# The adapter stage written out batch by batch, the initial semaphore values given by four engines, and the first expert's weight split moved to ScalarE and POOL during the selection

## The reference

```python
h = relu(einsum('bsh,bha->bsa', x, W1[lang]) + b1[lang])
x = x + einsum('bsa,bah->bsh', h, W2[lang]) + b2[lang]
n = (x - mean) * rsqrt(var + 1e-5) * gamma[lang] + beta[lang]
S = swapaxes(softmax(einsum('bse,ke->bsk', n, Wg)), 1, 2)
G, I = top_k(S, 128)          # tokens of each expert and batch
```

## Time and profile before

| | |
|---|---|
| Median of 3 runs | 1161.78 us (1161.07 to 1163.18) |
| Profiled execution | 1164.59 us, its span 1162.9 us |
| PE busy | 943.9 us, 81% |
| DVE busy | 746.9 us, 64% |
| POOL busy | 655.6 us, 56% |
| ACT busy | 469.0 us, 40% |

### The profile page before, as it was taken

One profiled execution on the slowest core, in us unless ns is written; L12 is line 12 of the kernel. 1 busy time (PEld: TensorE's weight loads), 2 busy tenths in 40 slices (PEclk: granted clock), 3 DMA queues, 4 the chain that ended last, 5 costly groups with the idle time before them and its releaser, 6 DMA issues. The chain is left out here.

```text
span 1162.9 us, 15224 instructions
## 1 busy us (share of the span) xinstructions
PE 943.9 (81%) x4616; PEld 683.2 (59%) x4616; DVE 746.9 (64%) x1525; ACT 469.0 (40%) x843; POOL 655.6 (56%) x480
## 2 busy tenths in 40 slices
PE   5975049999999999999457999888777888888870
PEld 2764039988998999886123554454454455555550
DVE  2443836666666676652487999999874766667620
ACT  1331126445545644543355657675522222222230
POOL 1010043545545554631899999999930477777771
PEclk9786569999999999998788999999976999999995
DMA  2355732445435433322222332442344599999957
GB/s 70 100 165 179 262 131 55 96 96 104 94 80 117 90 90 78 47 36 103 42 83 109 120 90 91 149 132 82 134 144 141 163 250 246 245 244 257 254 80 153
DMA packets 90450, 151.22 MB, mean 130 GB/s; under 512 B 15816, under 2 KB 72848, under 8 KB 87248
## 3 DMA queue, kind: packets, MB, share of 16 engines
q1 hardware_dynamic: 55184, 95.46, 25.9%
q0 software_dynamic: 25104, 39.86, 18.5%
q10 hardware_dynamic: 10096, 15.10, 3.9%
HBM read 115.37 MB, written 43.42 MB: 137 GB/s over the span
## 5 line engine op out<-in xcount | busy, mean ns | idle before, releaser
L843 ACT ACTIVATE h_raw<-bank,b 128x512 f32<-128x512 f32 x128 | 88.1, 688 | 169.4 <-PE bank L1600 167.1
L1188 DVE TENSOR_TENSOR h_lo<-h_raw,h_hi 128x512 fp32r<-128x512 f32 x128 | 87.2, 692 | 94.9 <-ACT h_hi L847 94.9
L1615 PE MATMUL bank<-w_hi,h_hi 128*128 128x256 f32 x512 | 144.5, 282 | 0.1
L1615 PE MATMUL bank<-w_lo,h_hi 128*128 128x256 f32 x512 | 142.4, 278 | 0.0
L1615 PE MATMUL bank<-w_hi,h_lo 128*128 128x256 f32 x512 | 142.3, 278 | 0.0
L1233 DVE TENSOR_TENSOR_SCAN body<-bank,body 128x512 f32<-128x512 f32 x112 | 130.9, 1211 | 16.7 <-POOL body L610 16.7
L584 POOL DMA_INDIRECT x_rows<-ob,put x64 | 110.6, 1728 | 27.5 <-issue 14.4
L618 POOL TENSOR_TENSOR acc<-acc,body 128x1024 f32<-128x1024 f32 x46 | 108.3, 2354 | 11.7 <-issue 8.2
L1600 PE MATMUL bank<-ex_hi,w_hi 128*128 128x512 f32 x256 | 100.7, 393 | 4.9 <-issue 4.9
L1600 PE MATMUL bank<-ex_hi,w_lo 128*128 128x512 f32 x256 | 101.8, 398 | 0.0
L1600 PE MATMUL bank<-ex_lo,w_hi 128*128 128x512 f32 x256 | 101.5, 396 | 0.0
(11 more groups left out here) (232 smaller groups left out, 2141.5 us busy)
## 6 DMA issues: line engine op xcount, KB each, us to landing
body<-in_mwp SPq DMA_DIRECT2D x46, 512.0 KB, 4.2
head<-in_mwp SPq DMA_DIRECT2D x18, 512.0 KB, 4.1
w1s<-in_fW SPq DMA_DIRECT2D x8, 1024.0 KB, 4.9
w2s<-in_fW SPq DMA_DIRECT2D x8, 1024.0 KB, 5.4
md<-m_rows SPq DMA_DIRECT2D x8, 1024.0 KB, 5.8
body<-m_rows SPq DMA_DIRECT2D x8, 1024.0 KB, 4.8
z_rows<-zrow SPq DMA_DIRECT2D x8, 640.0 KB, 7.1
xt<-in_x SPq DMA_DIRECT2D x8, 512.0 KB
```

The costliest lines, as they stand in the source:

```text
L843: A.activation(h1_raw[f % 4][:, :], bank[:, 2 + f % 4, :], ACT.Gelu_apprx_tanh, bias=b1_0[:, bass.ds(e, 1), f]).then_inc(b_h, 1)
L1188: V.tensor_tensor(h1_lo[:, f, :], h1_raw[f % 4][:, :], h1_hi[:, f, :].bitcast(F32), ALU.subtract).then_inc(b_lo, 1)
L1615: o = T.matmul(rows4(6)[:, j, :], x[:, f, rows], w[q][:, f * H:(f + 1) * H], start=(f == 0 and n == 0), stop=(f == FT0 - 1 and n == 2))
```

## The change

In the adapter stage the loops are gone: every engine has the steps of the 8 batches written out. TensorE's order becomes hidden(b), logits(b-2), adapted(b), input transposes(b+1), back transposes(b-1). VectorE's becomes logits copy(b-2), add and statistics(b), normalise(b), with the row bases of the indices computed in batch 2. ScalarE's becomes ReLU(b), copy of the transposes(b+1), gamma and beta(b-1), store(b-1). The loads of a batch are counted by two semaphores: `a_x` for the tokens, for which the input transposes wait, and `a_in` for the six small tensors, for which hidden waits. The increments of a counter `tally` (`settle`), for which nothing waits, are gone in this stage.

The credits are given by four engines: VectorE the 19 of the a_ semaphores, ahead of everything else it does; ScalarE the 18 of b_, behind its first two DMAs; TensorE the 47 of c_, ahead of its first wait; POOL the 16 of e_, behind its constants.

For the first expert, ScalarE writes the high parts right behind the Exp, ahead of the 22 loads, and POOL subtracts for the low parts, ahead of its wait for the index tables.

```diff
-        a_in = [sem(f"a_in{p}", 16 * 7) for p in range(2)]
+        a_x = [sem(f"a_x{p}", 16) for p in range(2)]
+        a_in = [sem(f"a_in{p}", 16 * 6) for p in range(2)]
...
+        def grant(eng, lo, hi):
+
+            for s, per in credited[lo:hi]:
+                eng.sem_inc(s, CREDIT * per)
...
             G = nc.gpsimd
-            for s, per in credited:
-                pool.sem_inc(s, CREDIT * per)
             G.memset(ident[:, :], 0.0)
...
             pool.drain().then_inc(consts, 1)
+            grant(pool, credits[2], len(credited))
...
-            with pool.Fori(0, B // 2) as i:
-                a_pow(i, 0)
-                a_pow(i, 1)
+            for b in range(B):
+                a_pow(b)
+
+
+            for first in (True, False):
+                src, hi, lo, up, split = ((w1s, w1_hi, w1_lo, b_w1h, b_w1l) if first else
+                                          (w2s, w2_hi, w2_lo, b_w2h, b_w2l))
+                pool.wait_ge(up, level(3))
+                G.tensor_tensor(lo[0][:, :], src[:, :], hi[0][:, :].bitcast(F32), ALU.subtract).then_inc(split, 1)
...
+            grant(act, credits[0], credits[1])
...
+            a_xT_out(0)
+            for b in range(B):
+                a_front(b)
+                if b + 1 < B:
+                    a_xT_out(b + 1)
+                if b:
+                    a_back(b - 1)
+                    a_store(b - 1)
+            a_back(B - 1)
+            a_store(B - 1)
...
             A.activation(lg0[:, :, :, :], lg0[:, :, :, :], ACT.Exp).then_inc(k_exp, 1)
+
+            for first in (True, False):
+                src, dst, came, split = ((w1s, w1_hi, b_w1, b_w1h) if first else (w2s, w2_hi, b_w2, b_w2h))
+                act.wait_ge(came, level(0, 16 if first else 32))
+                for n in range(4):
+                    A.activation(dst[0][:, n * 512:(n + 1) * 512], src[:, n * 512:(n + 1) * 512], ACT.Copy).then_inc(split, 1)
...
+            grant(dve, 0, credits[0])
             V.memset(zeros[:, :], 0.0).then_inc(zeros_set, 1)
...
+            for b in range(B):
+                if b > 1:
+                    a_logits(b - 2)
+                a_front(b)
+                if b == 2:
+                    row_bases()
+                a_norm(b)
+            a_logits(B - 2)
+            a_logits(B - 1)
...
+            grant(pe, credits[1], credits[2])
             pe.wait_ge(ident_set, 1)
...
+            a_xT_in(0)
+            for b in range(B):
+                a_hidden(b)
+                if b > 1:
+                    a_logits(b - 2)
+                a_adapted(b)
+                if b + 1 < B:
+                    a_xT_in(b + 1)
+                if b:
+                    a_backT(b - 1)
+            a_logits(B - 2)
+            a_backT(B - 1)
+            a_logits(B - 1)
```

More of the change, by code:

```diff
@@ L749, in a_store @@
                 act.wait_ge(a_nrm, level(b))
[L750 to L768, removed]
+                act.dma_start(n0_rows[b * S:(b + 1) * S, :].rearrange("(t p) c -> p t c", p=P), nrm[p][:, :, :]).then_inc(a_stored[p], 16)
+            a_xT_out(0)
[6 more added lines that the diff above has]
+                    a_store(b - 1)
@@ L809, in _ @@
             assert n == N_LOADED1
[L812 to L816, removed]
             WC = CT * FF0 // 4
@@ L1063, in a_norm, with a_logits, row_bases @@
                 o.then_inc(a_nrm, 1)
-            def a_logits(h, p):
-                b = 2 * h + p
+            def a_logits(b):
                 dve.wait_ge(a_lgm, level(b))
[L1068 to L1088, removed]
+                V.tensor_copy(lg0[:, b, :, :].rearrange("p t e -> p (t e)"), bank[:, 7, 0:TT * E0]).then_inc(a_lg, 1)
+            def row_bases():
+                dve.wait_ge(consts, 1)
+                V.tensor_scalar(rowbase[:, :], rowbase[:, :], -S, None, ALU.bitwise_and)
+                dve.drain()
+                V.tensor_copy(rowbase_f[:, :], rowbase[:, :])
+                dve.drain()
+                V.tensor_scalar(rowbase_f[B * E0:P, :], rowbase_f[B * E0:P, :], float(S // 2 - B * S), None, ALU.add)
+            for b in range(B):
[7 more added lines that the diff above has]
+            a_logits(B - 1)
             lgf = lg0[:, :, :, :].rearrange("p b t e -> p (b t) e")
@@ L1134, in _ @@
             dve.drain().then_inc(k_tab, 1)
[L1137 to L1140, removed]
-                V.tensor_tensor(lo[0][:, :], src[:, :], hi[0][:, :].bitcast(F32), ALU.subtract).then_inc(split, 1)
             WC = CT * FF0 // 4
@@ L1495, in _, with a_xT_in @@
             T = nc.tensor
+            grant(pe, credits[1], credits[2])
             pe.wait_ge(ident_set, 1)
             pe.wait_ge(loaded0, 16 * N_CONST0)
-            def a_xT_in(h, p):
-                b = 2 * h + p
-                pe.wait_ge(a_in[p], level(h, 16 * 7))
+            def a_xT_in(b):
+                p = b % 2
+                pe.wait_ge(a_x[p], level(b // 2, 16))
                 pe.wait_ge(a_xT, level(b - 1))
@@ L1507, in a_xT_in, with a_hidden @@
                 o.then_inc(a_xTm, 1)
-            def a_hidden(h, p):
-                b = 2 * h + p
+            def a_hidden(b):
+                p = b % 2
+                pe.wait_ge(a_in[p], level(b // 2, 16 * 6))
                 pe.wait_ge(a_xT, level(b))
@@ L1523, in a_adapted, with a_backT @@
                 o.then_inc(a_ad, 1)
-            def a_backT(h, p):
-                b = 2 * h + p
+            def a_backT(b):
+                p = b % 2
                 pe.wait_ge(a_nrm, level(b))
@@ L1542, in a_logits @@
                 o.then_inc(a_lgm, 1)
-            def a_both(h, p, last=False):
-                a_hidden(h, p)
-                a_backT(*prev(h, p))
-                a_adapted(h, p)
-                if not last:
-                    a_xT_in(*nxt(h, p))
-                a_logits(*prev(h, p))
-            def a_first():
-                a_xT_in(0, 0)
-                a_hidden(0, 0)
-                a_adapted(0, 0)
-                a_xT_in(0, 1)
-            def a_last():
-                a_backT(B // 2 - 1, 1)
-                a_logits(B // 2 - 1, 1)
-            adapters(pe, a_first, a_both, a_last)
+            a_xT_in(0)
+            for b in range(B):
+                a_hidden(b)
[9 more added lines that the diff above has]
+            a_logits(B - 1)
             pe.wait_ge(consts, 1)
```

62 lines of the change are left out of this document (28 added, 34 removed).

## The result

The changed kernel took 1132.39 us (4 runs, 1131.0 to 1132.99), the kernel before 1162.48 (4 runs, 1161.07 to 1168.4) beside it: ratio 0.9733, 95% interval 0.9700 to 0.9765. I had forecast 1138.3, a ratio of 0.980 to the 1161.78 of that time, and a range of 1132 to 1150. As a ratio its lower end is 0.9744, and the measured 0.9733 lies just under it. The direction and the three places were right, the gain was called too small. Over all occasions the runs of the kernel before lay between 1154.8 and 1170.7, so the closeness of the four runs on either side says little.

The account below looks back on a forecast made before the run. Everything waits for the expert stage's first product at 162.59 us, so gains before it count in full. 19.2 in the adapters plus 4.3 at the hand-over make 23.5, taking the median 1161.78 to 1138.3; range with rivals 1132 to 1150.

Parts of the forecast that it names:

- y(0) to y(1): Adapter stage, interval between the first two batches' adds: 10.3 us, allowing up to two batches for the clock's first rise.
- The start: Start of the adapters: first transposes wait for the tokens alone, at 7.7 instead of 10.39, 2.7 us gained (0 to 3).
- The cadence: Adapter batches in the new order: 7.7 us on TensorE with the clock up, taken as 8.0 (7.7 to 9.5).
- The third limit: Adapter stage, SP's loads of the tokens: the loop round them takes 15.9 us for two batches, 8.0 each.
- Once up the clock should stay up: Adapter stage: without the wait for a normalisation the clock stays up to the stage's end, five intervals of 8.0 us.
- The tail: From y(7) to the selection: 12.5 us instead of 14.38, by row bases moved (-0.67) and half the clock gain (-1.2).
- The hand-over: Index lists to first product: index copy, first gather, hand-over and last gather shorter, -4.3 us (-2.2 to -4.5).
- The rest: Behind the first product: nothing seen tied to another clock, so no change, 1000.3 us.
- rival 1: Adapter stage: the clock is late or falls again, two more batches at 13.4 instead of 7.7, +11.4 us, 1149.7; chance 0.17.
- POOL did not slow the loop: Selection: a rival had POOL's subtractions block VectorE's loop of max, find and replace, 9.4 us, 1147.7; chance 0.05.
- the clock never stayed down through the stage: Adapter stage: a rival had the clock down throughout, making the kernel slower, +11.1 us, 1172.9; chance 0.03.
- the loads did not set the pace: Adapter stage: a rival had the loads set the pace, 9.5 us a batch, 7.5 us more, 1145.8; chance 0.08.

Follow-up runs that it names:

- e5: The changed kernel measured and profiled again without any edit, against the kernel before: ratio 0.9768, median 1134.81 us.
- e12: The changed kernel a third time without any edit, against the kernel before: ratio 0.9771, median 1136.49 us.
- e3: The changed kernel with POOL giving all initial values again and the first expert's split in its old place (adapter part alone), against the kernel before: ratio 0.9816, 1143.84 us.
- e11: The changed kernel with tokens loaded ahead of the language id and TensorE's 47 initial values given by POOL, against the kernel before: ratio 0.9763, 1137.45 us.
- e4: The changed kernel with the old order of steps on TensorE, ScalarE and VectorE, all else kept, against the kernel before: ratio 0.9874, 1150.25 us.
- e6: The kernel before once more without any edit, for its profile: 1164.03 us (one run).
- e1: The kernel before with only the first expert's split moved (high parts behind the Exp, low parts on POOL), against the kernel before: ratio 0.9950, 1156.76 us.
- e8: The changed kernel with unread products, input transposes(b+1) between hidden and adapted, logits(b-2) last, language id read earlier, against the kernel before: ratio 0.9843, 1142.51 us.
- e10: Like e9, but TensorE's order is hidden(b), input transposes(b+1), adapted(b), back transposes(b-1), logits(b-2); against the kernel before: ratio 0.9743, 1134.62 us.
- e2: The kernel before with only the initial values spread over four engines, against the kernel before: ratio 1.0002, 1163.18 us.
- e9: The changed kernel with tokens loaded ahead of the language id, TensorE's 47 values given by POOL and a few unread products, against the kernel before: ratio 0.9693, 1127.98 us.

## Why the prediction came out too small

By its own steps, before the profile of after:

| step | forecast | first profile | e5 | e12 |
|---|---|---|---|---|
| first transposes | 7.7 | 8.31 | 8.31 | 8.31 |
| y(0) | 19.0 | 17.86 | 19.64 | 17.86 |
| y(0) to y(1) | 10.3 | 6.70 | 9.29 | 6.71 |
| y(1) to y(2) | 9.7 | 9.56 | 7.65 | 8.45 |
| y(2) to y(7) | 40.0 | 40.01 | 41.19 | 41.01 |
| y(7) to the selection | 12.5 | 14.03 | 13.80 | 14.03 |
| selection starts | 91.5 | 88.16 | 91.57 | 88.06 |
| hand-over | 15.7 | 15.23 | 15.1 | 15.2 |
| rest | 1000.3 | 996.0 | 992.4 | 998.0 |

**The step that failed** is "I read its rises as coming out of hidden matmuls and allow up to two batches for the first: that puts y(0) to y(1) at 10.3". In the first profile the clock was up when the adapted matmuls of batch 0 began (1.99 us at 15.83, against 3.62 in the earlier trace rows), so y(0) came 1.1 early and y(1) another 3.6: an interval of 6.70 instead of 10.3. e5 is the case that I had priced, and its stage starts at 91.57, where I had put 91.5; that this is so close is luck, since its intervals miss by up to 2 us either way (table). The same kernel shows both cases. The early rise is there in after, e12, e3 and e11, which have the new order, and not in e5, e4 and the four profiles with the old loops, though up to the first adapted matmuls TensorE has the same steps in all of them; whether more than chance is in that stays open. The two averages behind this step are a tenth off, which cancels: its terms give 9.5 or 11.2, evenly 10.4, and 7.7 and 11.5 give 9.6, not 9.7.

**The start** was forecast 0.6 too early: the load of the tokens began at 3.61, where I had 4.2, but took 4.7 us to land, not 3.5. TensorE's increments, "at double they take 7.5", cost that double; they were free by 0.3 us only.

**The base** was a fast one: the selection starts at 110.70 in it, at 113.92 in e6 and 113.38 in e1, which have the same adapters and the same start. Against these the stage gained more than the 22.54 of the first pair.

**The cadence** of 7.65 with the clock up is what the order was to give (7.7). The third limit was mis-sized: the 8.0 came from the loads, and they did not bind (no wait for them from batch 3 on); what lifts the mean over 7.65 is the clock. That y(2) to y(7) took 40.01 against 40.0 is luck, a term for the loads that was not there in place of falls of the clock that were. "Once up the clock should stay up" was wrong. It fell with TensorE busy all the time, during logits and adapted back to back (instructions first, then busy time and granted clock by stretch, columns as in the earlier trace rows):

```profile
45.60 1.95 PE L1518 MATMUL bank<-wg,yT 128*128 128x8 f32 x16
...
47.41 2.03 PE L1501 MATMUL bank<-w2c,hT 65*128 65x256 f32 x8
```

```profile
46.00:48.00 2.00, 2.00 (x17) 1.95 (x18) 1.48 (x5) 0.39 (x1) 0.47 (x1) 1.00 0.88 263
48.00:49.10 1.10, 1.10 (x7) 0.97 (x6) 0.00 (x0) 0.00 (x0) 0.00 (x0) 1.00 0.52 130
49.10:50.00 0.90, 0.90 (x6) 0.81 (x5) 0.53 (x1) 0.00 (x0) 0.00 (x0) 0.55 0.14 2
```

This fall cost only 1.3 us (adds 8.93 apart instead of 7.65); the first, at 25.3 with a wait of 0.40 for the tokens ahead of it, 1.9 (9.56). In both the two groups of transposes followed, and the clock was up again within 0.5 us of the start of the next hidden (28.21 and 52.72). In the old order adapted, transposes, logits and hidden passed at the lower level, 13.7 us each time, from 38.9 and from 79.9 on (the earlier trace rows lie in these two). Why it rises sooner in the new order was not tested.

What the engine did before a fall is the same in most cases. Of the nine falls in the adapters of after, e5 and e12, eight came during adapted matmuls right behind logits or within 0.4 us behind them; the one at 25.3 came in a batch without logits. Where other steps stood between logits and adapted matmuls, the clock stayed up much longer: from 47.1 to 88.0 in e4, 35.3 to 86.5 in e8, 43.6 to 81.1 in e10; those of e8 and e10 ahead of that, at 28.5 and 29.9, came behind waits for the tokens of 3.21 and 2.73 us.

**The tail** was 1.5 us dearer: I had counted half of the last transposes and logits at the full clock, and both ran at the lower one in the first profile (1.95 and 3.58), since the clock fell a third time at 73.1 and stayed down.

**The hand-over** gained 4.8 instead of 4.3: the first gather takes 1.28, not 0.97, but the last gather of the four lands 2.9 after its start instead of 4.6.

**The rest**, "I see nothing" later tied to another clock, was a term put at nothing: no shift of its mean can be told, but one execution is off from the next by several us there, 990.8 to 1002.9. Of the 31 us of the first measurement some 4 are of this kind; the three measurements together stand at 27 to 31. The first profile's span is 8.2 us below the forecast's (1131.2 against 1162.9 - 23.5 = 1139.4): 3.3 in the stage, where the early clock in batch 0 gave 4.7 and the tail took 1.5 back, 0.5 at the hand-over, and 4.3 in the rest. With the rest at 1000.3 the ratio would have lain inside the range, as it does in e5 and e12. Of the rivals, the clock fell again as rival 1 says, but at 1.3 to 1.9 us a time and not at the 5.7 of its price; POOL did not slow the loop, the clock never stayed down through the stage, and the loads did not set the pace.

## What to carry to other kernels

Order an in-order engine's list so that the step that waits for the longest chain comes last, and a two-batch-old step fills another wait: that was worth about half of the gain (ratio 0.9874 without it, 0.977 with it), three to five times a batch what writing the loops out gave. Look for what an engine's serial set-up work delays, and price it on the engine that is to do it, since the same increment cost twice as much on TensorE; here moving it gave nothing by itself (e2), because another wait ended just behind it. Where the parts of a change sum to less than its profile shows, take the same kernel's profile twice before looking for a mechanism.

## What was not expected of the hardware

Semaphore increments in a row came 0.15 us apart on TensorE, 0.08 on POOL and 0.09 on VectorE. TensorE's granted clock fell from 1.00 to 0.50 while the engine was busy without a gap (46.00 to 49.10 of the first profile); what it did was logits, 16 products of 8 columns, and the adapted matmuls. And products that nobody reads brought it up in time for work behind them: in e9 four of them, from 2.34 us on, gave a hidden of 1.90 instead of 3.65, and five behind the first row transposes, with five more ahead of these, a first instruction of the experts' first product of 0.47 instead of 0.77.
